# Last attention of a four-layer network on one core: transposes and divisions of the mixed rows placed behind a step's first score block

## What is computed

```
Q = rope(split_heads(x @ Wq)); K = rope(split_heads(x @ Wk)); V = split_heads(x @ Wv)
scores = einsum('bhqd,bhkd->bhqk', Q, K) / sqrt(8)
scores = where(causal, scores, -inf)
attn = softmax(scores, axis=-1)
out = einsum('bhqk,bhkd->bhqd', attn, V).transpose(0, 2, 1, 3).reshape(B, S, D)
return out @ Wo
```

## Time and profile before

| | us |
|---|---|
| median of 3 runs | 5603.11 |
| lowest and highest run | 5591.78, 5604.20 |
| profiled execution, its own time | 5578.07 |
| its span, first to last instruction | 5576.2 |
| mean granted TensorE clock over the span | 0.932 |
| TensorE busy | 4761.3 (85%) |
| VectorE busy | 3824.3 (69%) |
| ScalarE busy | 2844.1 (51%) |
| GpSimd busy | 2601.5 (47%) |

### The profile page before, as it was taken

One profiled execution on the slowest core, in us unless ns is written; L12 is line 12 of the kernel. 1 busy time (PEld: TensorE's weight loads), 2 busy tenths in 40 slices (PEclk: granted clock), 3 DMA queues, 4 the chain that ended last, 5 costly groups with the idle time before them and its releaser, 6 DMA issues. The chain is left out here.

```text
span 5576.2 us, 143468 instructions
## 1 busy us (share of the span) xinstructions
PE 4761.3 (85%) x57069; PEld 3327.6 (60%) x57103; DVE 3824.3 (69%) x9101; ACT 2844.1 (51%) x6227; POOL 2601.5 (47%) x3093
## 2 busy tenths in 40 slices
PE   7699999999999999999999999853376999945886
PEld 3366666666666666666666666633364666523665
DVE  7677777777777777777777777566726777776442
ACT  2256666666666566666666666521014666641332
POOL 4477667776667667766776676501120000011000
PEclk9899999999999999999999999976587999966997
DMA  0211111111111111111111100000210000000012
GB/s 20 70 28 25 25 34 36 25 25 34 35 24 25 34 36 25 25 34 35 26 25 33 25 21 21 13 22 17 64 52 18 2 2 1 4 22 13 27 27 54
DMA packets 312164, 150.61 MB, mean 27 GB/s; under 512 B 146143, under 2 KB 301003, under 8 KB 311243
## 3 DMA queue, kind: packets, MB, share of 16 engines
q1 hardware_dynamic: 309451, 137.20, 10.2%
q0 software_dynamic: 2048, 4.20, 0.3%
HBM read 101.10 MB, written 27.41 MB: 23 GB/s over the span
## 5 line engine op out<-in xcount | busy, mean ns | idle before, releaser
L1435 POOL TENSOR_TENSOR loc_a<-loc_a,loc_b 128x512 f32<-128x512 f32 x768 | 978.8, 1277 | 229.2 <-DVE loc_b L1511 228.6
L1123 PE MATMUL psum<-loc_wqk,loc_xt 128*128 128x512 f32 x1536 | 828.2, 621 | 15.6 <-issue 4.9
L1186 PE MATMUL psum<-loc_m,xn_rows 128*128 128x128 f32 x6144 | 821.9, 277 | 4.6 <-DVE y_rows L1543 3.0
L1307 ACT ACTIVATE loc_sq<-psum 128x512 f32<-128x512 f32 x768 | 455.4, 593 | 679.3 <-PE psum L1123 678.7
L1460 POOL TENSOR_TENSOR loc_a<-loc_a,loc_rn 128x512 f32<-128x512 f32 x768 | 786.6, 1048 | 0.1
L1186 PEld LDWEIGHTS psum<-loc_m,xn_rows 128*128 128x128 f32 x6144 | 752.4, 192 | 47.8 <-issue 45.0
L1507 DVE TENSOR_TENSOR loc_a<-psum,loc_rope 128x512 f32<-128x512 f32 x768 | 524.2, 683 | 337.4 <-ACT loc_sq L1307 323.6
L1467 POOL TENSOR_TENSOR xn_cols<-xn_cols,loc_rec 128x512 f32<-128x512 f32 x384 | 394.1, 1047 | 683.8 <-DVE loc_rec L1538 683.4
L1344 ACT COPY xn_rows<-psum 128x512 f32<-128x512 f32 x768 | 411.9, 588 | 220.8 <-PE psum L1174 217.1
L1511 DVE TENSOR_TENSOR loc_b<-psum,loc_rope 128x512 f32<-128x512 f32 x768 | 521.9, 680 | 0.0
L1515 DVE TENSOR_REDUCE loc_n<-loc_sq 128x8 f32<-128x512 f32 x768 | 518.3, 675 | 0.0
(11 more groups left out here) (372 smaller groups left out, 8728.9 us busy)
## 6 DMA issues: line engine op xcount, KB each, us to landing
loc_x<-loc_shifted SPq DMA_DIRECT2D x192, 256.0 KB, 4.0
loc_shifted<-y_rows SPq DMA_DIRECT2D x144, 64.0 KB
loc_wqk<-in_L_ffn_Wqkv SPq DMA_DIRECT2D x24, 256.0 KB, 3.8
x_rows<-y_rows SPq DMA_DIRECT2D x96, 64.0 KB
x_rows<-y_rows SPq DMA_DIRECT2D x96, 63.5 KB
moe_w<-in_L_ffn_W SPq DMA_DIRECT2D x16, 256.0 KB, 4.6
l3a_qk<-l3a_rot SPq DMA_DIRECT2D x16, 256.0 KB, 2.1
grp_w<-in_L_ffn_W SPq DMA_DIRECT2D x16, 256.0 KB, 4.2
```

Source lines behind the costliest of these rows:

```text
L1123: nc.tensor.matmul(ring("p", i, unit), xt[:, b % 2, t * P:(t + 1) * P], wqk[:, unit * 512:(unit + 1) * 512], start=True, stop=True).then_i ...
L1186: last = nc.tensor.matmul(y_bank[:, 0:P], u[:, i % 2, h // 2, h % 2, :], m[:, h, :], start=(h == 0), stop=(h == HEADS - 1))
L1307: nc.scalar.activation(sq[:, g % 2, :], ring("p", i, unit), ACT.Square).then_inc(sem["squared"], 1)
L1435: nc.gpsimd.tensor_tensor(part, part, b_[:, g % 2, :], ALU.add).then_inc(sem["added"], 1)
```

## The change

In TensorE's program `turn_mixed(n - 4)` stood ahead of the step's loop over blocks; it now stands in the loop, behind `scores(n - 1, 0)` and ahead of `project(n, "w")`. In VectorE's program `divide(n - 4)` goes likewise behind `tops(n - 1, 0)` and ahead of `rope_part(n, "w")`. The table of PSUM uses is unchanged, and so are the programs of ScalarE, GpSimd and SP.

```diff
@@ -2687,11 +2687,11 @@
 
                 for n in range(LAST_STEP):
                     now = lambda lag: 0 <= n - lag < NB
-                    if now(4):
-                        turn_mixed(n - 4)
                     for b in range(3):
                         if now(1):
                             scores(n - 1, b)
+                        if now(4) and b == 0:
+                            turn_mixed(n - 4)
                         if now(0) and b < 2:
                             project(n, "wr"[b])
                         if now(4) and b == 2:
@@ -2810,11 +2810,11 @@
 
                 for n in range(LAST_STEP):
                     now = lambda lag: 0 <= n - lag < NB
-                    if now(4):
-                        divide(n - 4)
                     for b in range(3):
                         if now(1):
                             tops(n - 1, b)
+                        if now(4) and b == 0:
+                            divide(n - 4)
                         if now(0) and b < 2:
                             rope_part(n, "wr"[b])
         for clear in (zero, zero_read, zero_top):
```

## The result

The changed kernel takes 5646.89 us (median of 4 runs, 5643.69 to 5650.72) against 5602.19 us (5591.78 to 5604.20) before: 44.7 us slower by the medians. The ratio is 1.0084 with a 95% interval of 1.0068 to 1.0100. Ratios here are estimated from the runs together with their interval; they are not quite the quotient of two medians. The profiled execution took 5647.43 us, with a span of 5645.6 us. It stands 69 us above the span of the profile of before, but 21.5 us of that lie ahead of the stage (its first projection starts at 5107.41 before and 5128.88 after): the profiled execution of before was a fast one. In the stage itself, from there to its end, it is 47.6 us.

The account below looks back on a forecast made before the run. TensorE was taken to bound the last attention's 21.45 us step, idle at the seam until ScalarE's store. Twelve steps gave +19.3 us, step 16 about -1, the clock +3: +21 to +22 on 5603.11, so 5625 us, range 5607 to 5644.

Parts of the forecast that it names:

- parts 1 to 4: Last attention's step, from block 0's start through reductions and division to "w" and the turned scores: +1.6 us a step.
- term (1): Block 0's masks at the seam wait for the qa/ka reads: start 5257.21, 0.9 us earlier than before; bounds 5256.2 to 1.04 later.
- The sign given for it: Profile after, last attention: full-clock steps would measure 23.0 us at clock 1.00.
- reads early: Rival: qa/ka reads land early at the seam, +0.6 us a step, step 22.1 us, total 5611 us; chance 0.11.
- Step 16: Last attention's step with divisions but no "w": block 0 and what follows gain about 1 us.
- The clock: TensorE at 1.2 GHz in the last attention: two more slow steps than before, 1.6 us each, +3 us.
- the clock falls in every step: Rival: "w" at 1.2 GHz costs 1.8 us more in all twelve steps; 5635 us, or 5643 with old falls; chance 0.13.

Follow-up runs that it names:

- the order behind the turned scores: Against the kernel before: transposes and divisions moved behind block 0's turned scores, bank table with them; 5642.01 us, with seven fillers at the seam 5607.50 us.

## Why the prediction was wrong

The direction was right, 5625 us was not, and 5646.89 us lies above the range.

**The order (parts 1 to 4): right where the reads are waited for.** It was put at +1.6 us a step, with a step of 23.05 us. With the clock held by fillers, the changed order has a clean step of 23.07 us, block 0's products to "w" 4.29 us (forecast: 5258.20 to 5262.49, 4.29), "w" to the turned scores 1.92 us (forecast 1.93), and the DMA as releaser of block 0. "w" comes 7.32 us behind the maxima's transposes (5281.44 to 5288.76), forecast 7.31 (5255.18 to 5262.49), so the landing taken from the first reads of the stage holds in that step. Over twelve steps, both orders with fillers and a clock of 0.99, it is 280.97 - 258.88 = 22.1 us, against 19.3 forecast. The missing 0.2 us a step are term (1) in the steps whose reads land later; 23.75 and 23.93 us are among the longest at full clock.

The sign given for it, 23.0 us at clock 1.00, never appears in the changed kernel itself. Its only two steps at full clock last 21.87 us. There block 0 follows the exponentials, as the prediction's "reads early" has it for a step of 22.1 us, because a slow step had just given the reads time to land. In the ten other steps the wait at the seam was 2.0 us on average where the prediction counted 1.5.

**Step 16: undersized.** It gained 3.8 us, not 1: before, it had spent much of its time at 1.2 GHz (clock 0.80), after, less (0.92).

**The clock: the step that failed.** "I count two more of them than before, +3 us" took the falls of before, one at a time and 1.6 us each, for the kind that would come. The twelve steps spent some 115 us at 1.2 GHz instead of 21. What fillers give back is 318.43 - 280.97 = 37.5 us after and 266.98 - 258.88 = 8.1 us before: +29.4 us where I had +3. The 51.5 us of the twelve steps thus split into 22.1 for the order and 29.4 for the clock. That the two add up is no check, as one is what the other leaves; the timed medians put the fillers' part after at 33 us instead of 37.5. Less the 3.8 us of step 16, the 51.5 give the 47.6 us of the stage in the profiles. The timed runs have 44.7 us.

**The rival "the clock falls in every step"** was the right one, with ten of twelve steps below a clock of 1.00, and it had 0.13. Its own times, 5635 and 5643, were too low because a fall was priced at one slow stretch of 1.8 us, from "w" to the turned scores. In the step shown above the mix and a part of block 1's products ran slow too: between "w" and block 1's products lie 8.46 us (5273.76 to 5282.22), and in the clean step 4.47 (5383.96 to 5388.43): 4.0 us for one fall. I argued against this rival from six steps with a gap of 1.6 us that kept the clock. They had one such gap, at the seam, with dense transposes behind it; the changed kernel has two, up to 2.7 us at the seam and up to 2.1 us behind the transposes, with block 0's 8-row products between them. Either gap alone was enough next to these products: with the gap behind the transposes gone or filled the clock was 0.82 to 0.89, with the seam filled 0.85, against 0.96 before. The argument took the steps of before as a sample of what a gap does and left out what runs next to it.

Beside this rival the prediction set a rule. The Trainium skill (TensorE: Matmul & The Clock Gate, "HAM oscillation — how this bites in real kernels") tells of a loop that waits for a DMA in every turn and is throttled again in every turn. Here it was ten turns of twelve, with waits shorter than those of the Trainium skill's example: no wait of TensorE in the twelve steps of the changed kernel is longer than 2.7 us.

## What to carry to other kernels

Before work is moved behind a block, look up which buffer the next piece takes and who must free it: here a reordering that fills one gap put four reductions and a division ahead of a projection through a two-bank ring. A gap of TensorE can cost more than its length; price it from what the slow clock makes of the whole stretch behind it (here some 10 us at 1.2 GHz for a gap of 2), and test it with filler products in a bank that is overwritten. When a wait for one engine is removed, find the wait that was hidden behind it: here the reads land at about the moment the store is over (in the step shown the store ends at 5268.14 and the masks start behind the reads at 5268.50), so that taking the store away won little.

## What the runs showed of the hardware

Filling one of two gaps did almost nothing at the seam (clock 0.85 against 0.82) and something behind the transposes (0.89), filling both gave 0.99. The same order with and without fillers differs by 34 us (the order behind the turned scores, 5642 and 5607 us), although the fillers are added work whose results are thrown away. Most falls before lasted about 3 us, most of those after about 10 us; in the step shown TensorE worked without a break from "w" on. Why they last longer is open. So is how much the thinness of the products and how much the standing still counts: no run changed the rows of the score products alone, and the gaps of the orders compared differ in length too. How soon the reads land behind their last issue is not one number: where TensorE waited for them it was mostly 2.4 to 2.9 us, but 1.8 to 1.9 us in the steps whose four issues took 2.1 to 2.9 us instead of 1.33.
